# A four-layer perceptron on TensorE: another tile-to-bank mapping for its 64x64 tiles, and its last matmul as four 32-column tiles

## What is computed

```python
nbr = neighbor_sum(gn(x))                 # 16 channels
h = elu(w1 @ repeat(nbr, 8))              # 64 hidden channels, layer 1 (weights summed over the repeats)
h = elu(w2 @ h); h = elu(w3 @ h); h = elu(w4 @ h)    # 64x64, layers 2 to 4
F = w5 @ h                                # then means over 4 groups, times 0.1: 16 channels
x = x + F_reduced
```

## Time and profile before

| what | value |
|---|---|
| median of 3 runs | 975.99 us (975.88 to 980.12) |
| the profiled execution | 984.4 us, span 982.6 us |
| mean granted TensorE clock | 0.893 |
| PE busy | 740.2 us (75%) |
| DVE busy | 682.5 us (69%) |
| ACT busy | 611.4 us (62%) |
| POOL busy | 150.7 us (15%) |

### The profile page before, as it was taken

How to read it: one execution, slowest core, us unless ns; L and a number is a source line. 1 busy time by engine, 2 the same in 40 slices (tenths; PEclk the granted TensorE clock), 3 DMA queues, 4 the chain that set the end, 5 groups by cost and what they waited for, 6 DMA issues and landing times.

```text
span 982.6 us, 9594 instructions
## 1 busy us (share of the span) xinstructions
PE 740.2 (75%) x3156; PEld 279.7 (28%) x3156; DVE 682.5 (69%) x963; ACT 611.4 (62%) x633; POOL 150.7 (15%) x228
## 2 busy tenths in 40 slices
PE   1759788878886978787888888888888766666663
PEld 1423443323232223323232333323333212221110
DVE  1635576869687868778787879787868677754441
ACT  0020115777668676867677777877767777777672
POOL 2030141204010131113010402040202010200000
PEclk9989798999999999999999999999979979696665
DMA  5425353030011201040104010300110010001001
GB/s 95 75 43 96 72 93 79 1 57 7 14 29 31 33 0 43 0 62 0 43 0 62 0 30 13 51 11 14 29 31 1 1 43 1 0 17 27 0 1 43
DMA packets 61070, 30.62 MB, mean 31 GB/s; under 512 B 4066, under 2 KB 60770, under 8 KB 61042
## 3 DMA queue, kind: packets, MB, share of 16 engines
q1 hardware_dynamic: 59296, 29.99, 16.5%
q10 hardware_dynamic: 1746, 0.27, 0.3%
HBM read 9.67 MB, written 8.39 MB: 18 GB/s over the span
## 4 chain that ended last, share of the span: by engine, by line
PE 29%; DVE 26%; ACT 25%; issue 8%; DMA 6%; SPq 3%; POOL 1%; DVEq 0%; ACTq 0%; POOLq 0%
ACT u L493 13%; ACT u L496 10%; PE pz L603 9%; DVE g L812 8%; PE pc L555 5%; PE po L617 4%; DVE g_last L812 3%; DMA halo<-y 3%; PE pz L590 3%; DMA xs<-in_x_dram 3%; DVE bn L736 3%; SPq L351 3%; DVE box_sum L848 2%; DVE box_sum L850 2%; PE pc L540 2%
## 5 line engine op out<-in xcount | busy, mean ns | idle before, releaser
L603 PE MATMUL pz<-g,wT 64*64 64x512 f32 x1536 | 227.4, 672 | 98.0 <-DVE g L812 96.2
L493 ACT ACTIVATE u<-pz,s_row 128x1024 f32<-128x1024 f32 x192 | 212.4, 1106 | 121.8 <-PE pz L603 121.8
L496 ACT ACTIVATE u<-u 128x1024 f32<-128x1024 f32 x256 | 270.7, 1057 | 8.1
L812 DVE SCALAR_TENSOR_TENSOR g<-pz,k_row,u 128x1024 f32<-128x1024 f32 x128 | 162.3, 1280 | 68.6 <-ACT u L496 68.4
L812 DVE SCALAR_TENSOR_TENSOR g<-pz,u 128x1024 f32<-128x1024 f32 x64 | 78.4, 1225 | 85.5 <-ACT u L496 85.5
L603 PEld LDWEIGHTS pz<-g,wT 64*64 64x64 f32 x1536 | 48.2, 141 | 247.3 <-issue 247.2
L493 ACT ACTIVATE u<-pz 128x1024 f32<-128x1024 f32 x64 | 64.9, 1014 | 83.0 <-PE pz L590 83.0
L736 DVE BATCH_NORM_STATS2 bn<-xs 128x6 f32 (+1 forms) x128 | 87.1, 688 | 31.8 <-DMA xs<-in_x_dram 21.9
L812 DVE SCALAR_TENSOR_TENSOR g_last<-pz,k_row,u 128x1024 f32<-128x1024 f32 x64 | 81.2, 1278 | 36.2 <-ACT u L496 36.2
L555 PE MATMUL pc<-y,t 128*128 128x512 f32 x192 | 101.4, 669 | 5.9 <-DVE t L321 4.9
L565 PE MATMUL pc<-y,t 128*128 128x512 f32 x192 | 96.5, 641 | 3.0 <-ACT y L466 2.6
(11 more groups left out here) (107 smaller groups left out, 655.6 us busy)
## 6 DMA issues: line engine op xcount, KB each, us to landing
halo<-y SPq DMA_DIRECT2D x96, 120.0 KB, 3.3
xs<-in_x_dram SPq DMA_DIRECT2D x8, 1024.0 KB
out_dram<-xs SPq DMA_DIRECT2D x8, 1024.0 KB
halo<-y SPq DMA_DIRECT2D x48, 8.0 KB, 2.7
g<-in_con_late_dram SPq DMA_DIRECT2D x1, 712.5 KB, 10.3
con<-in_con_early_dram SPq DMA_DIRECT2D x1, 272.5 KB, 16.0
u<-in_L_conv_w_dram ACTq DMA_DIRECT2D x6, 16.0 KB, 8.4
g<-in_L_conv_w_dram ACTq DMA_DIRECT2D x2, 32.0 KB, 3.9
```

Of the source, the lines that this page charges most:

```text
L493: act.activation(u[:, pair, :], pz[:, pair, :], ACT.Relu, scale=-1.0, bias=s_row[:, l - 1:l] if l else 0.0).then_inc(relu_done, 1)
L496: act.activation(u[:, pair, :], u[:, pair, :], ACT.Exp, scale=-1.0).then_inc(exp_done, 1)
L603: last = pe.matmul(pz[half, to, :], wT[rows, l, rows], g[rows, of, :], start=True, stop=True)
L812: dve.scalar_tensor_tensor(out=elus(l)[:, pair, :], in0=pz[:, pair, :], scalar=k_row[:, l - 1:l] if l else 1.0, in1=u[:, pair, :], op0=ALU ...
```

## The change

In `hidden_layer` the same four matmuls of a pair are mapped otherwise: what comes from bank a stays where it is (upper to upper, lower to lower), and what comes from bank b goes to the other half of bank b. So after three such layers bank a is as after layer 1, and bank b has its halves exchanged. Both pixel rows of a bank stay in it. That makes `last_layer` four matmuls of 32 columns each, one for each bank, without accumulation, where it had four of 64 columns that were added in twos. `w5T` has 32 columns for that, filled at places that follow the exchanged halves.

```diff
-        w5T = sb("w5T", [P, 2, HID])
+        w5T = sb("w5T", [P, 2, 32])
...
-                    for rows, to in ((top, a), (bottom, b)):
-                        for half, of in ((top, a), (bottom, b)):
-                            last = pe.matmul(pz[half, to, :], wT[rows, l, rows], g[rows, of, :], start=True, stop=True)
+                    for rows, across in ((top, bottom), (bottom, top)):
+                        pe.matmul(pz[rows, a, :], wT[rows, l, rows], g[rows, a, :], start=True, stop=True)
+                        last = pe.matmul(pz[across, b, :], wT[rows, l, rows], g[rows, b, :], start=True, stop=True)
...
-                for odd in range(2):
-                    for h in range(2):
-                        last = pe.matmul(po[HID * h:HID * h + HID, :], w5T[:, odd, :], g_last[:, 2 * h + odd, :],
-                                         start=odd == 0, stop=odd == 1)
+                for m in range(M):
+                    last = pe.matmul(po[32 * m:32 * m + 32, :], w5T[:, m % 2, :], g_last[:, m, :], start=True, stop=True)
...
-                        at = 2 * C * p + C * odd
+                        at = C * (p ^ odd)
```

More of the change, by code:

```diff
@@ L667, in _ @@
                 pe.matmul(po[:, 64 + l:65 + l], wT[:, 1 + l, :], const("one"), start=True, stop=True)
-            for odd in range(2):
-                for h in range(2):
-                    last = pe.matmul(po[HID * h:HID * h + HID, 67:68], w5T[:, odd, :], const("one"), start=odd == 0, stop=odd == 1)
+            for m in range(M):
+                last = pe.matmul(po[32 * m:32 * m + 32, 67:68], w5T[:, m % 2, :], const("one"), start=True, stop=True)
             last.then_inc(setup_pe, 1)
```

## The result

The changed kernel takes 984.71 us (median of 20 runs, 978.09 to 988.78); the kernel before, run beside it, takes 978.09 us (20 runs, 973.18 to 980.34). The ratio is 1.0069, 95% interval 1.0052 to 1.0086: slower, where 971.7 us and a small gain were forecast. Three runs far above the others of their kernel belong to a slower state and are left out of medians, clocks and ratios: one of e8 (1420.26 us) and two of the kernel before beside e5 to e8 (2285.7 and 986.73 us).

What follows compares the result with a forecast made beforehand. No engine alone was taken as the bound (PE, DVE, ACT 29, 26, 25%). Savings of 7.55 us less 3.2 us of clock loss, net 4.3, bring 984.4 to 980.1; less 8.4 from profile to median, 971.7 us, range 966 to 978.

Steps and rivals of the forecast that it cites:

- rival D: Rounds 2 to 7: less PE work also lowers the clock, 0.9 us per half-clock stretch; 974 to 982 us, chance 10%.
- (1): Layers 2 to 4: the exchanged tiles cost 0, groups staying at 1.09 us; upper bound 0.85 us more a group.
- Rival A: Layers 2 to 4: two row tiles in one bank take turns, 0.85 us more a group; about 1041 us, chance 10%.
- (2): Last matmul: four 32-column tiles run side by side, 1.94 to 1.09 us a group, 27 us of PE saved.
- Rival B: Last matmul: 32-column tiles don't all run side by side, staying at 1.94 us; 976.0 us, chance 8%.
- The savings on the path: Shorter last matmul where PE holds the path: 4.25 us, 1.6 us in round 7, 1.7 us at the end, 7.55 us.
- conv of the first kind: Five parts with L555 and L558 behind the last matmul; PE holds the chain, 0.85 us saved each, 4.25 us.
- The 1.6 us of round 7: Parts at 803.60 and 851.45: layer 2 starts 0.8 us earlier in each; round 7's other two parts save 0.
- (3): Round 8: PE idles more, the clock rises later, layer 2 loses 0.81 us in each of four parts, 3.2 us.
- Rival C: Round 8: the clock rises as before, so the whole 7.55 us stay; 968.4 us, chance 20%.
- The base: Whole kernel: the profiled 984.4 us lies 8.4 us above the runs' median, a difference carried over to the forecast.
- mine: Whole kernel: the main forecast of 971.7 us, with 969.5 to 974 as its own range, chance 52%.

Runs made afterwards that it cites:

- e8: e7 plus unread matmuls filling PE's waits in the parts of rounds 7 and 8 without a conv: 959.23 us, ratio 0.9832 to the kernel before.
- e5: Changed kernel with its last matmul done twice in rounds 1 to 6 alone: 977.22 us, ratio 0.9997 to the kernel before.
- e1: Kernel before with only the new mapping of layers 2 to 4, keeping the old last matmul: 977.19 us, ratio 1.0007.
- e4: The kernel before run again, nothing changed, for a second profile and its spread: 977.23 us, ratio 0.9997.
- e9: The changed kernel run again, nothing altered, for its spread and a second profile: 984.18 us, ratio 1.0101 to the kernel before.
- e10: Changed kernel plus one unread matmul behind the last matmul in third and fourth parts of rounds 1 to 6: 979.98 us, ratio 1.0036 to the kernel before.
- e2: Kernel before with only the new 32-column last matmul, on the old mapping, output rows misplaced: 986.04 us, ratio 1.0110.
- e6: Changed kernel with its last matmul done twice in rounds 7 and 8 alone, the very last one single: 980.95 us, ratio 1.0046 to the kernel before.
- e3: Changed kernel with its last matmul done twice over everywhere: 974.63 us, ratio 0.9998 to the kernel before.
- e7: Changed kernel, last matmul once in first parts of rounds 2 to 6 and at the very end, twice elsewhere: 973.91 us, ratio 0.9968 to the kernel before.
- e11: Kernel before, last matmul unchanged, with e8's unread matmuls in parts of rounds 7 and 8 without a conv: 962.54 us, ratio 0.9867.

## Why the prediction was wrong

Wrong were the sign and the range; even rival D, which had the right cause, ended at 982 us. Step by step:

- **(1) Layers 2 to 4 at no cost: right.** Groups take 1.09 us at full clock as before (503.56 to 504.65 in the lines below, the first and the last instruction of one), and e1 is at 1.0007. Rival A is out. The Trainium skill (TensorEngine Tiling (Array Packing), Gotcha 1: PSUM Pressure) forbids different row tiles in one bank at one time; these tiles write different partitions of it, and neither a wait nor a loss shows here.

```profile
503.56 0.61 PE L602 MATMUL pz<-g,wT 64*64 64x512 f32 x1 [0.71 <-DVE g L809]
...
504.06 0.59 PE L603 MATMUL pz<-g,wT 64*64 64x512 f32 x1
```

- **(2) The last matmul at 1.09 us: right**, 1.07 us, so four streams of 128 rows do run side by side. Rival B is out. The Trainium skill's 2.38 times for three tiles (TensorE: Matmul & The Clock Gate, Measured speedup vs the span model) would, by the prediction's estimate, have made it 1.38 us, and the trace is below that. The saving on PE was larger than the 27 us, 35 to 38 us, since many groups run at half clock.
- **The savings on the path: right in size, but only where the clock stayed the same.** The five first parts with a conv of the first kind took 139.1 us in e4 and 134.8 us in e9, with the same 13.7 us at half clock in both: 4.3 us, forecast 4.25. e10, with no filling in these parts, has 134.8 too. But that is the favourable case: in the changed kernel, e2 and e6 the same parts took 139.6, 138.1 and 141.4 us, with 20 to 27 us at half clock. The last group went from 3.68 to 1.94 us, 1.74, forecast 1.70. The 1.6 us of round 7 did not come: its parts at 801 and 849 went from 22.89 to 22.52 and from 22.85 to 22.28, but e4 has 22.52 and 22.58 there without the change, and the other two, put at 0, took 24.42 and 25.43 us, where the first profile has 23.70 and 24.96 and e4 24.17 and 24.99. The whole round took 94.3 to 94.6 us before, in e1 and in e4, and 94.1 to 94.7 in the changed kernel, e2 and e9.

```profile
969.51 1.94 PE L616 MATMUL po<-g_last,w5T 128*32 128x512 f32 x8 [3.63 <-DVE g_last L809]
```

- **(3) The clock in round 8: right in place and size.** 0.8 us lost a part, forecast 0.81. Rival C did not come. The clock did more than rise later: in the second part it is at 0.50 through the whole of layer 2, and full only from 910.4 to 913.7, 3.3 us where the row of before has 6.70. That the loss stayed at 0.8 us is in part luck, since the later groups ran at half clock already before. Round 8 with the end took 110.0 us in the mean of before, e1 and e4, and 112.0 in that of the changed kernel, e2, e5, e9 and e10: 2.0 us lost, where 3.2 less 1.7 were forecast. The windows in the changed kernel:

```profile
897.50:901.00 3.50, 1.86 (x8) 0.12 (x8) 1.23 (x1) 3.41 (x4) 0.00 (x0) 0.50 0.00 0
901.10:905.00 3.90, 3.88 (x16) 0.58 (x16) 1.88 (x2) 2.42 (x3) 0.00 (x0) 0.50 0.00 0
905.10:920.00 14.90, 6.87 (x32) 1.24 (x32) 7.59 (x6) 10.82 (x11) 0.00 (x0) 0.61 0.00 1
```

- **The step that failed is rival D: the clock also falls in rounds 2 to 7.** I gave it 10%, with "five bring the time back to 976, eleven to over 980.9", and counted 0 us for the second to fourth parts as "something later hides the saving". The time was hidden there, but PE's idle stretch was not harmless: it had grown from 0.82 to 1.69 us in the fourth parts, and that is where the new half-clock stretches follow, 1.1 to 2.2 us each (23.9 to 24.2 us against 22.0 to 22.8), where D had priced one at 0.9. Of the 24 fourth parts of rounds 1 to 6 with less work on PE (after, e2, e6, e9) eight are such; of the 54 with the work in place (before, e1, e3, e4, e5, e7, e8, e10, e11) none is. The idle stretch in front of L526 is 0.83 us or less in all of the 54. In the 24 it is 1.01 to 1.70 us, and all eight falls are among the fifteen with 1.65 us or more; the other seven of these kept the full clock, and what decides between them stays open. e5 shows that most of the loss sits in rounds 1 to 6: the ratio falls from 1.0069 or 1.0101 to 0.9997, some 7 to 10 us. I had argued against D from one stretch of round 8, where the clock stayed full although PE worked 3.08 of 6.70 us. That row showed only that such a stretch can happen, and right behind it L603 is at half clock again, 1.98 us at 907.84.
- **The base.** I carried the 8.4 us between profile and median over, and that hid a second warning. The profile ahead of the prediction is slower than all 20 runs of its kernel, with half-clock stretches in rounds 2 to 4 (L617 at 3.2 to 3.56 us), while e4's has L617 mostly at full clock (median instruction 593 ns). The spread of one kernel goes with the clock: over 74 runs of the kernel before the time falls by 4.3 us for each 0.01 of mean clock (correlation -0.64), and over 27 of the changed one by 2.6 us (-0.70). Between the two kernels the mean clock differs by 0.033 (0.904 and 0.871), so by these slopes 9 to 14 us, an estimate from a correlation that e5 and e6, with one clock and two times, show to be rough. Less the 7.55 us forecast as saved that is 1 to 7 us lost; measured were 6.6 us, and in e9 7.5.
- **The chances.** All of C and four in ten of mine are 0.41; D's range, 974 to 982, adds nothing below 971.1 us, so 0.42 was a little too much.

What is shown: the loss comes with the shorter last matmul (e1, e2), and added work that nobody uses takes it away, wholly (e3, e5) or in part (e10). In the fourth parts the half-clock stretches come and go with PE's idle stretch. For a profile as a whole it is less clear: 173 us at half clock in e3, 218 in e5 and 235 in e10, against 237 and 228 in the changed kernel.

How the loss divides can be read only roughly, from sums over rounds 1 to 6 of four profiles with less work on PE there (changed kernel, e2, e6, e9) and six with the work in place (before, e1, e3, e4, e5, e11), as means:

| parts | us, less work | us, work in place | at half clock, less work | at half clock, work in place |
|---|---|---|---|---|
| first | 165.4 | 165.7 | 24.7 | 16.5 |
| second | 137.2 | 136.8 | 6.0 | 4.0 |
| third | 179.8 | 179.3 | 25.6 | 25.6 |
| fourth | 138.0 | 135.3 | 6.8 | 0.0 |
| all | 620.4 | 617.2 | 63.1 | 46.2 |

By these means the fourth parts lose 2.8 us, and the first parts lose by half clock what the shorter matmul saves them: 0.3 us are left (0.8 in rounds 2 to 6, where 4.25 were forecast). With the 2.0 us of round 8 that makes 5.2 us, near the 6.6 and 7.5 us between the medians. The sum over rounds 1 to 6 of a single profile varies from 615.8 to 624.9 us and from 610.4 to 622.9, so how a median run's loss divides stays open.

## What to carry to other kernels

In this kernel time saved on TensorE off the path became idle time, and idle time some of the clock of the matmuls that are on the path. So ask of each shortened group how long PE now stands still behind it, not only what hides it. Before counting a small gain, look at how a kernel's own runs spread with the mean granted clock; where a hundredth of clock goes with several microseconds, as here, a change of PE's load by 4% is not small. Where PE waits for other engines, unread matmuls within its waits can be worth more than the tuning of the real ones: they took 1.3% off the kernel before (e11) and 1.4% off e7's (0.9968 to 0.9832).

## What the runs showed of the hardware that was not expected

- More work made the kernel faster: e3 does 27 us more of PE work at full clock than the changed kernel and is 0.7% faster (1.2% faster than e2 beside it). The Trainium skill, TensorE: Matmul & The Clock Gate, HAM oscillation — how this bites in real kernels, says that waits between bursts of matmuls bring the clock down again; the trace agrees, with the clock at 0.50 from 343.8 us on behind a wait of 1.69 us, and not at 0.82 us; but seven of the fifteen fourth parts with a wait of 1.65 us or more kept the full clock.
- Two row tiles (upper rows to the upper half, lower rows to the lower half) wrote one PSUM bank side by side at no price that shows: 1.09 us a group, ratio 1.0007 (0.9984 to 1.0029).
- Four 32-column tiles that each read 128 rows of float32 ran as fast as four 64x64 tiles that each read 64: 1.07 and 1.09 us.
- In round 8 of e8 the granted clock was 0.94 with PE busy 75.44 of 97.80 us, against 0.57 with 60.06 of 111.40 us in the changed kernel.
